# Attention on Trainium2: the far key blocks' relative term as two rows of the turned scores

## The reference, cut to what matters

```
q, k, v = projections of layernorm(x), 16 heads of 8 values
dist    = clip(i - j, -128, 128) + 128              # i query, j key
scores  = (q . k + q . rel_emb[dist]) / sqrt(8)
local   = softmax(scores) @ v
combined = gate * local + (1 - gate) * (elu(q)+1) M / (elu(q)+1) z
x = x + combined @ Wo.T + bo
```

## Time and profile before

| what | us |
|---|---|
| median of 3 runs | 2716.86 |
| the profiled execution | 2697.04 |
| its span, first to last instruction | 2693.7 |
| TensorE busy in the span | 2108.9 (78%) |
| VectorE, ScalarE, GpSimd busy | 1545.9, 1420.6, 1128.7 |
| attention without its first and last sequence | 787 to 2002 |

### The profile page before, as it was taken

How to read it: one execution, slowest core, us unless ns; L and a number is a source line. 1 busy time by engine, 2 the same in 40 slices (tenths; PEclk the granted TensorE clock), 3 DMA queues, 4 the chain that set the end, 5 groups by cost and what they waited for, 6 DMA issues and landing times. The chain is left out here.

```text
span 2693.7 us, 49339 instructions
## 1 busy us (share of the span) xinstructions
PE 2108.9 (78%) x16104; PEld 1469.7 (55%) x16104; DVE 1545.9 (57%) x4196; ACT 1420.6 (53%) x2765; POOL 1128.7 (42%) x1594
## 2 busy tenths in 40 slices
PE   5556896621899999999999999999999675789660
PEld 4444674510556666566666666666666554567540
DVE  7564554533566666666666666666764555555441
ACT  3544564411466666665666666666664343566440
POOL 1665003475444443454444444444441265400566
PEclk9777998865689999998999999998999777899885
DMA  5244885622878877787778778887783113488662
GB/s 140 96 155 164 246 238 170 186 85 49 228 215 236 217 223 226 218 232 211 213 220 235 222 216 237 224 226 211 215 235 94 32 43 119 144 243 238 201 197 76
DMA packets 382770, 496.56 MB, mean 184 GB/s; under 512 B 43956, under 2 KB 316212, under 8 KB 382516
## 3 DMA queue, kind: packets, MB, share of 16 engines
q1 hardware_dynamic: 326644, 308.21, 42.7%
q0 software_dynamic: 53248, 184.07, 21.0%
q10 hardware_dynamic: 2624, 1.13, 0.2%
HBM read 252.56 MB, written 214.95 MB: 174 GB/s over the span
## 5 line engine op out<-in xcount | busy, mean ns | idle before, releaser
L1358 DVE CUSTOM_DVE_ANT_0 at_junk<-at_ps_s,at_rel 128x512 bf16<-128x512 f32 x1024 | 665.0, 687 | 285.3 <-PE at_ps_s L959 237.3
L1132 ACT ACTIVATE at_probs<-at_ps_t 128x512 f32<-128x512 f32 x1024 | 559.8, 597 | 111.2 <-PE at_ps_t L944 96.6
L1141 ACT COPY at_src<-at_ps_r 128x512 f32<-128x512 f32 x512 | 301.5, 589 | 429.6 <-PE at_ps_r L971 381.8
L944 PE MATMUL at_ps_t<-tab_ident,at_rel 128*128 128x128 f32 x3328 | 504.3, 293 | 0.0
L517 POOL DMA_INDIRECT ffn_zg<-rows_z,rows_home x256 | 249.4, 974 | 474.6 <-issue 394.1
L944 PEld LDWEIGHTS at_ps_t<-tab_ident,at_rel 128*128 128x128 f32 x3328 | 377.6, 147 | 72.3 <-issue 9.0
L718 DVE TENSOR_TENSOR ffn_h<-ffn_silu,ffn_ps_gate 128x512 f32<-128x512 f32 x248 | 170.4, 687 | 351.6 <-ACT ffn_silu L480 264.3
L507 POOL DMA_INDIRECT rows_x<-ffn_xe,rows_index x256 | 254.4, 994 | 252.7 <-ACT ffn_xe L459 171.4
L480 ACT ACTIVATE ffn_silu<-ffn_ps_mid 128x512 f32<-128x512 f32 x248 | 148.9, 600 | 389.8 <-PE ffn_ps_gate L319 226.9
L959 PE MATMUL at_ps_s<-at_ks,at_qs 24*128 24x512 f32 x1024 | 317.0, 520 | 34.0 <-DVE at_mx L1358 28.8
L985 PE MATMUL at_ps_v<-at_probs,at_v 128*32 128x256 f32 x4096 | 339.8, 405 | 0.2 <-ACT at_probs L1132 0.2
(11 more groups left out here) (196 smaller groups left out, 3436.0 us busy)
## 6 DMA issues: line engine op xcount, KB each, us to landing
at_band<-at_src POOLq DMA_DIRECT2D x256, 574.0 KB, 4.7
at_rel<-at_band SPq DMA_DIRECT2D x512, 143.5 KB, 3.7
ffn_w_expert<-rows_w SPq DMA_DIRECT2D x92, 768.0 KB
ffn_xg<-rows_x SPq DMA_DIRECT2D x92, 256.0 KB
rows_z<-ffn_y SPq DMA_DIRECT2D x92, 256.0 KB
rows_x<-ffn_zero SPq DMA_DIRECT2D x46, 256.0 KB
at_rel<-at_band SPq DMA_DIRECT2D x64, 128.0 KB, 3.3
at_rel<-at_band SPq DMA_DIRECT2D x64, 127.5 KB, 3.3
```

What stands on the lines that cost most here:

```text
L944: ins = pe.matmul(ps_t[:, i, HALF * n + P * l:HALF * n + P * (l + 1)], rel[:, c % RREL, l, 2 * hp + i, kb * P:(kb + 1) * P], ident[:], sta ...
L1132: act.activation(probs[:, kp, 2 * hp + i].rearrange("p n q -> p (n q)"), ps_t[:, i, :], ACT.Exp).then_inc(exp_done.sem, 1)
L1141: act.copy(src[:, l, 2 * hp:2 * hp + 2, 0:BAND], ps_r[:, :, 0:BAND]).then_inc(qr_out.sem, 1)
L1358: dve.tensor_tensor_reduce(out=junk[:, i, :], in0=ps_s[:, i, :], in1=rel[:, c % RREL, l, h, :], scale=1.0, scalar=-3e38, op0=ALU.add, op1= ...
```

## The change

It replaces part of the transposes by rows of the matmul, and moves three pieces of work:

- `add_turned` leaves out the pieces with `kb > qb + 1` too: steps 2 and 3 of an even item have 2 transposes for 8. An even item has 20 where it had 32, the odd ones keep 20.
- For these pieces `far` enters as two more rows of the turned product: `far` in its float32r rounding and the rest, against rows of ones in `ks`. GpSimd makes both (`far_rows`) in even slots, in columns 8 to 23 of `mx`; they are turned with the maxima, VectorE copies 24 rows for 8, and SyncE issues three DMAs for one in `maxima_in` of even items. TensorE's `turn_maximum` of even items waits for `far_done`. Key block 2 of an even item is cut into two matmuls of 128 columns, since only one of its two query blocks is far.
- The normalising goes from VectorE at (7, 0) to GpSimd in slot 6 (the first sequence stays on VectorE).
- The four statistics go from (5, 0) to two at (5, 1) and two at (5, 3).
- `stack` goes part by part: the first part of q needs only `q_hi` and goes at slot 1, the second and third at slot 2; the keys' high parts at (3, 1) and (4, 0), the low one at (4, 1). There are as many DMAs as before.

```diff
     def spread(eng, b, a, parts, to, rings):
         r = b % R2
-        for m in range(HG * n, HG * n + HG):
-            h, a = divmod(m, PART)
+        for h in range(HG):
             at = 32 * h + HD * a
...
-    QUERIES_IN = ((2, 0), (2, 1), (3, 0))
-    KEYS_IN = ((3, 1), (4, 0), (4, 1))
+    QUERIES_IN = (((1, 0), 0), ((2, 0), 1), ((2, 1), 2))
+    KEYS_IN = (((3, 1), 0), ((4, 0), 2), ((4, 1), 1))
...
+                        if half_of(c) == 1 or kb < 2:
+                            pieces = ((near, 0, HALF),)
+                        elif kb == 2:
+                            pieces = ((every, 0, P), (near, P, HALF))
+                        else:
+                            pieces = ((every, 0, HALF),)
+                        for m, (rows, low, high) in enumerate(pieces):
+                            pe.matmul(ps_t[:, i, HALF * n + low:HALF * n + high], ks[rows, r, s, kb * P:(kb + 1) * P],
+                                      qs[rows, r, s, first + low:first + high], start=(n == 0 and m == 0), stop=False,
+                                      skip_group_check=True)
...
-                            if kb < qb - 1:
+                            if kb < qb - 1 or kb > qb + 1:
                                 continue
...
                 pe.wait_ge(max_done.sem, max_done.at(j, 2 * HG))
+                if half_of(c) == 0:
+                    pe.wait_ge(far_done.sem, far_done.at(c // 2, 2))
...
+            def far_rows(c):
+                j, n = c, c // 2
+                m_turned.wait(pool, j, -1)
...
+                value = far[:, c % RREL].rearrange("p l h a -> p h l a")
+                high, low = (mx[:, c % R2, 2 * HG * x:2 * HG * (x + 1)].rearrange("p (h l a) -> p h l a", h=HG, l=2)
+                             for x in (1, 2))
+                pool.wait_ge(pad_done.sem, pad_done.at(j, 4))
+                pool.tensor_copy(high.bitcast(F32R), value).then_inc(far_done.sem, 1)
+                pool.wait_ge(far_done.sem, far_done.at(n, 1))
+                pool.tensor_tensor(low, value, high, ALU.subtract).then_inc(far_done.sem, 1)
...
+            def normalise(b):
...
+                pool.wait_ge(xT_turned.sem, xT_turned.at(b, 0))
+                for t in range(QPB):
+                    row = b * QPB + t
+                    ins = pool.tensor_scalar(xn[:, t, :], X[:, row, :], mean[:, row, :], rstd[:, row, :],
+                                             ALU.subtract, ALU.mult)
...
+                if item(c + 2) is not None and half_of(c + 2) == 0:
+                    far_rows(c + 2)
                 if item(c + 4) is not None:
                     send_band(c + 4, 0)
                 if coming(c) is not None:
                     project(c)
+                if after_coming(c) is not None and c % PER == NORMALISE_SLOT:
+                    normalise(after_coming(c))
...
-                sp.dma_start(to.bitcast(F32), mrow[:, c % R2, :].bitcast(F32)).then_inc(m_ring.sem, 16)
+                for x in range(EXTRA if half_of(c) == 0 else 1):
+                    at = ((ROW + x) * R2 + par_of(c)) * SETS * S + set_of(c) * S + HALF * half_of(c)
+                    to = bass.AP(qs[:].tensor, at, [[32 * R2 * SETS * S, HG], [1, HALF]])
+                    sp.dma_start(to.bitcast(F32), mrow[2 * HG * x:2 * HG * (x + 1), c % R2, :].bitcast(F32)).then_inc(m_ring.sem, 16)
...
-                dve.tensor_copy(mrow[:, c % R2, :], misc[0:2 * HG, 0:P]).then_inc(m_row.sem, 1)
+                dve.tensor_copy(mrow[:, c % R2, :], misc[0:2 * HG * EXTRA, 0:P]).then_inc(m_row.sem, 1)
```

More of the change, by code:

```diff
@@ L767, in attention_phase @@
     ROW = PART * HD
+    EXTRA = 3
     HALF = 2 * P
@@ L849, in attention_phase @@
         m_turned, m_row = ring("m_turned", 1), ring("m_row", 1)
-        m_in = [ring(f"m_in{r}", 16) for r in range(R2)]
+        m_in = [ring(f"m_in{r}", 16 * (EXTRA if r == 0 else 1)) for r in range(R2)]
+        far_done = ring("far_done", 2)
         t_done, exp_done = ring("t_done", 2 * HG), ring("exp_done", 2 * HG)
@@ L926, in scores_turned @@
                     exp_done.wait(pe, j, 2 * k + i - 1)
-                    rows = slice(32 * h, 32 * h + ROW + 1)
-                    q = qs[rows, r, s, HALF * half_of(c):HALF * (half_of(c) + 1)]
+                    near = slice(32 * h, 32 * h + ROW + 1)
+                    every = slice(32 * h, 32 * h + ROW + EXTRA)
+                    first = HALF * half_of(c)
                     for n in range(2):
                         kb = 2 * kp + n
-                        pe.matmul(ps_t[:, i, HALF * n:HALF * (n + 1)], ks[rows, r, s, kb * P:(kb + 1) * P], q,
-                                  start=(n == 0), stop=False, skip_group_check=True)
+                        if half_of(c) == 1 or kb < 2:
[8 more added lines that the diff above has]
+                                      skip_group_check=True)
             def add_turned(c, k):
@@ L1298, in maxima_in @@
                 m_ring, n = pair_ring(m_in, c)
-                at = (ROW * R2 + par_of(c)) * SETS * S + set_of(c) * S + HALF * half_of(c)
-                to = bass.AP(qs[:].tensor, at, [[32 * R2 * SETS * S, HG], [1, HALF]])
-                sp.dma_start(to.bitcast(F32), mrow[:, c % R2, :].bitcast(F32)).then_inc(m_ring.sem, 16)
+                for x in range(EXTRA if half_of(c) == 0 else 1):
+                    at = ((ROW + x) * R2 + par_of(c)) * SETS * S + set_of(c) * S + HALF * half_of(c)
+                    to = bass.AP(qs[:].tensor, at, [[32 * R2 * SETS * S, HG], [1, HALF]])
+                    sp.dma_start(to.bitcast(F32), mrow[2 * HG * x:2 * HG * (x + 1), c % R2, :].bitcast(F32)).then_inc(m_ring.sem, 16)
             def stack(c, half):
                 b, place = coming(c), (c % PER, half)
-                if place in QUERIES_IN:
-                    n = QUERIES_IN.index(place)
-                    if n == 0:
-                        sp.wait_ge(qlo_done.sem, qlo_done.at(b, 1))
-                        t_done.wait(sp, c - c % PER, 0)
-                    if b > 0 or n != 1:
-                        spread(sp, b, n, (q_hi, q_hi, q_lo), qs, q_in)
-                elif place in KEYS_IN:
-                    n = KEYS_IN.index(place)
-                    if n == 0:
-                        sp.wait_ge(klo_done.sem, klo_done.at(b, 1))
-                    if b > 0 or n != 1:
-                        spread(sp, b, n, (k_hi, k_lo, k_hi), ks, k_in)
+                for at, a in QUERIES_IN:
+                    if at == place and (b > 0 or a != 1):
+                        if a == 0:
+                            sp.wait_ge(qhi_done.sem, qhi_done.at(b, 1))
+                            t_done.wait(sp, c - c % PER, 0)
+                        elif a == 2:
+                            sp.wait_ge(qlo_done.sem, qlo_done.at(b, 1))
+                        spread(sp, b, a, (q_hi, q_hi, q_lo), qs, q_in)
+                for at, a in KEYS_IN:
+                    if at == place and (b > 0 or a != 2):
+                        if a == 0:
+                            sp.wait_ge(khi_done.sem, khi_done.at(b, 1))
+                        elif a == 1:
+                            sp.wait_ge(klo_done.sem, klo_done.at(b, 1))
+                        spread(sp, b, a, (k_hi, k_lo, k_hi), ks, k_in)
             def slot(c):
@@ L1330, in slot @@
                     stack(c, 1)
-            sp.wait_ge(cleared.sem, 4)
-            minus = bass.AP(ks[:].tensor, ROW * R2 * SETS * S, [[32 * R2 * SETS * S, HG], [1, R2 * SETS * S]])
-            sp.dma_start(minus.bitcast(F32), glob[:, 0, :]).then_inc(minus_in.sem, 16)
+            sp.wait_ge(cleared.sem, 5)
+            for x in range(EXTRA):
+                signs = bass.AP(ks[:].tensor, (ROW + x) * R2 * SETS * S, [[32 * R2 * SETS * S, HG], [1, R2 * SETS * S]])
+                sp.dma_start(signs.bitcast(F32), glob[:, 0 if x == 0 else 2, :]).then_inc(minus_in.sem, 16)
             for i in range(4):
@@ L1453, in leave @@
                     dve.tensor_tensor(rows, misc[:], rows, ALU.add).then_inc(y_done.sem, 1)
-                    dve.wait_ge(y_done.sem, y_done.at(b, 1))
-                    for t in range(QPB):
-                        row = b * QPB + t
+                elif place in STATS_OUT:
+                    if place == STATS_OUT[0]:
+                        dve.wait_ge(y_done.sem, y_done.at(b, 1))
+                    for t in range(2):
+                        row = b * QPB + 2 * STATS_OUT.index(place) + t
                         dve.bn_stats(STATS[:, bass.ds(row, 1), :].rearrange("p a d -> p (a d)"),
@@ L1465, in slot @@
                         values_out(c - 1)
-                    if after_coming(c) is not None and (c % PER, k) == NORMALISE:
-                        normalise(c)
+                    if after_coming(c) == 0 and (c % PER, k) == NORMALISE:
+                        normalise_first()
                     if coming(c) is not None:
```

42 lines of the change are left out of this document (22 added, 20 removed).

## The result

The kernel with the change takes 2686.26 us (median of 6 runs, 2673.18 to 2694.16), the kernel before in the same comparison 2717.45 (2706.34 to 2719.67). The ratio is 0.9891, 95% interval 0.9861 to 0.9921: about 30 us faster, where 2575 was forecast and the range began at 2500 and ended at 2650. The sign was right, the size was not: 30 us came where the sum had 130.

The account below looks back on a forecast made before the run. TensorE was taken to set the pace. Transposes 71, queries 36, normalising 49 and statistics 4, less 30 given back, made 130 us; from 2697 that left 2567, plus 8 for the profiled run's draw: 2575, range 2500 to 2650.

Parts of the forecast that it names:

- Queries in: Slot 4: laying q's third part in sooner ends the band product's 2.4 us wait whole, 36 us gained.
- Transposes: Even items' steps 2 and 3: 768 transposes fewer save 92 us, cut matmuls add 21, net 71 us gained.
- Normalising: Slot 7: moving VectorE's four instructions to GpSimd in slot 6 ends a stall of 3.5 us a sequence, 49 us gained.
- Given back: Slot 6: later-landing maxima DMAs cost 16 us and late band copies into `src` 14, together 30, between 0 and 60.
- The maxima's 16 us: Slot 6: three DMAs for one make the last land 1.1 us later, costing 16 us.
- The cut matmuls: Even items: key block 2 cut in two adds 256 matmuls at 0.083 us, 21 us lost.
- The prediction's own sign of being wrong: A sequence over 82 us with a DMA share near 0.85, or TensorE idle in every even item.
- the rival behind it: The DMA engines take over: only a 0.85 share can be held, sequence 80.7 us, median 2620; chance 0.18.
- More than the terms: Whole kernel: nothing is given back and the clock rises, 2497 us; chance 0.17.
- Transposes don't pay: Even items: the pieces or a wait for VectorE eat what the transposes leave, 2623 us; chance 0.08.
- slower by the maxima in each even item: The maxima's DMAs become the wait of every even item; 4 us each makes 2777 us; chance 0.04.
- The four statistics: Four instructions leave the step where VectorE also adds the output: 4 us gained in all, between 0 and 10.

Follow-up runs that it names:

- all three parts and no far rows: Kernel before with queries laid in early head by head, normalising on GpSimd and far transposes left out, nothing in their place: 2610.07 us, ratio 0.9655.
- the best version: Changed kernel with the queries stacked head by head in slots 1, 2, 2: 2634.95 us, ratio 0.973 against the kernel before.

## Why the prediction was wrong

**The first step that failed is Queries in.** It priced the stacking by its place and count ("the 24 DMAs of a sequence stay 24") and gave the new order no price. The early places are worth 41 us from before (36 forecast). The new order costs 55 us there (1.0052 against 0.9849) and 43 in the changed kernel, so the part alone is not a gain of 36 but 14 us slower. It also didn't look for what would be late next in slot 4: the maxima's rows, 42.0 us in 30 times.

**The second is the sum, which adds Transposes and Normalising as if they were independent.** The 49 us of Normalising are for a stall that needs VectorE's four instructions beside GpSimd's fill. Without the transposes the two no longer meet, and the removal alone takes 2.0 of the 3.5 us. By the slots 38 of the 52 us that the parts lose together are this stall, counted twice.

**Given back** was 30 us and its bound 60. The mechanism for the bands was named (a copy in `src` waits for a landing), with 4.7 us as a fixed landing time. The landing is not fixed, it went to 5.4, and ScalarE's wait from 29.2 to 136.4. In the changed kernel with another order the landing is 4.7 to 5.0 and the wait 62.2 to 77.8, so about half of it belongs to the order too. The maxima's 16 us in it were wrong the other way; one DMA or three make no difference that can be told. What makes up the 14 us that are missing beyond slot 7 stays open, and they are within the noise.

**Transposes.** The removal is 72 us, forecast 92, and it owes some 30 of these to slot 7 (2.0 us in 15 sequences). In its own steps, even items' 2 and 3, it takes 3.6 us a sequence in the kernel with nothing in their place, an estimate of 57 us in 16; waits that grew elsewhere, that for q above all, take some back. Four of these eight steps fall by 0.58 to 0.66 us, 0.11 for a transpose and nearly the 0.12 of the prediction; the other four fall by 0.21 to 0.32. Step 2 of slot 0 in that kernel shows why for one of them:

```profile
1351.50 0.44 PE L944 MATMUL at_ps_t<-tab_ident,at_rel 128*128 128x128 f32 x2
1352.12 0.66 PE L1068 MATMUL at_misc<-tab_ident,at_oc 128*128 128x128 f32 x4 [0.18 <-DVE at_local L1430]
```

The two transposes are followed after 0.62 us and not after 0.27, because what comes next needs the PSUM bank `misc`, which VectorE has to empty first. Step 2 of slot 2 has the same gap at the same bank. The prediction asked whether another engine ends the shortened steps and took the answer from rows 4, where only the turning of the maxima goes through that bank. The steps 3 of slots 4 and 6 weren't followed.

The cut matmuls are best read in one place. Slot 6, step 2, before and then after (TensorE, start and duration; x6 are six matmuls):

```profile
1468.37 0.51 PE L931 MATMUL at_ps_t<-at_qs,at_ks 25*128 25x256 f32 x4
1468.81 1.09 PE L944 MATMUL at_ps_t<-tab_ident,at_rel 128*128 128x128 f32 x8
```

```profile
1449.18 0.64 PE L997 MATMUL at_ps_v<-at_probs,at_v 128*32 128x256 f32 x8
...
1449.98 0.62 PE L942 MATMUL at_ps_t<-at_qs,at_ks 27*128 27x128 f32 x6
1450.52 0.44 PE L956 MATMUL at_ps_t<-tab_ident,at_rel 128*128 128x128 f32 x2
1450.89 0.64 PE L997 MATMUL at_ps_v<-at_probs,at_v 128*32 128x256 f32 x8
```

The step is 1450.89 - 1449.18 = 1.71 us, 1.57 forecast. Four take 0.44 here and six 0.54. In step 2 of slots 0, 2 and 4 it is 0.33 and 0.43 to 0.44. So a piece costs 0.05 us and not 0.083, 13 us for 21, near the lower bound. The estimate of 27 us that the prediction made from the Trainium skill (TensorE: Matmul & The Clock Gate, "The mechanism") isn't borne out by these rows either.

**Normalising.** The cause and the place were right: slot 7 lost 3.4 us with this part alone (3.5 forecast), and without the fill beside them the four instructions take 1.12 us on VectorE itself. What was wrong is that the sum could still win it all beside the removal. GpSimd in slot 6 after:

```profile
1449.76 0.73 POOL L1227 DMA_DIRECT2D at_band<-at_src  x1 [0.54 <-POOL at_src L1221]
1450.46 3.17 POOL L1286 TENSOR_SCALAR at_xn<-X,at_moments,at_rstd 128x128 f32<-128x128 f32 x4
1453.56 0.20 POOL L1220 COPY at_far<-at_src 128x4 f32<-128x4 f32 x1
```

Four instructions take 3.17 us where 1.6 to 2.4 was given, so they fill more than the idle 2.81 of the earlier trace rows, and the copy behind starts with no gap. What this costs wasn't parted.

**Rivals.** The prediction's own sign of being wrong, a sequence over 82 us with a DMA share near 0.85, is what came: 83.8 us and 0.86. But the rival behind it (0.18, 2620) took 0.85 for the most that can be held, and that was wrong. About half of the rise in the share is that the bytes of a packet took longer (9% more busy for 4% more bytes); the kernel with all three parts and no far rows runs 64 us faster than the change at the same 0.86, with 243 GB/s (780 to 1940). "More than the terms" didn't come, and the mean clock stayed 0.95. Its mechanism is there all the same: 0.97 with the normalising alone, 0.98 with the three parts and no far rows. "Transposes don't pay" and "slower by the maxima in each even item" are both refuted, by 0.9736 for the transposes alone and by the kernel with one DMA.

**The sum again**, in us and by the ratios: 72 (removal) + 41 (early queries) + 35 (normalising) - 52 (missing when the three are together) - 20 (far rows) = 76 for 73 measured of the best version, and 43 less for the part order makes 33 where 30 were measured. The 52, the 20 and the 43 were themselves taken as differences between these kernels, so that this comes out is no check of it. Against the forecast 130, the part order (43), what is missing beyond the 14 given back for the bands (38), the removal (20) and the normalising (14) are short, and the far rows (17) and the queries (5) are better. The four statistics, 4 us in the sum, weren't tested alone.

## What to carry to other kernels

An edit that only reorders DMAs isn't free: price where each one lands against the one ahead of it, by the duration of its packets and by the landing times of the other queues' transfers, not by count and bytes. Before terms are added, ask of each stall whether another term already ends it: a stall that needs two instructions to meet goes with any edit that shifts one of them. And split an edit that changes both a place and an order; in the kernel before the one was worth 41 us and the other cost 55, and together they looked like little.

## What the runs showed of the hardware

- Stacking DMAs of 2048-byte packets that go in turn to partitions 0 and 32, then 64 and 96: 142 to 144 ns a packet, 116 to 126 in the other orders. The rest of the traffic pays too: a band landed in 5.4 us and not in 4.7 to 5.0.
- Six transposes of 128x128 fewer in a step are 0.65 us where TensorE sets it, 0.11 each for a duration of 293 ns in the profile, and 0.2 to 0.3 where it waits for something else.
- Two matmuls of 128 columns for one of 256 cost 0.05 us more (0.54 us for 0.44 with two cuts, slot 6).
- Four VectorE instructions of 128x128 took 1.12 us alone and 3.74 beside a GpSimd copy of 2.31.
- GpSimd's subtract-and-multiply with an operand for each partition takes 0.85 us for 128x128 (812 to 898 ns over 60), more than a quarter of the 1.59 of its 128x512 instruction.
